# Graph attention on one core: 16 key blocks of each batch element turned by VectorE and DMA in place of TensorE

## The reference

```python
h = jnp.maximum(_layernorm(x, axis=-1), 0.0)
q = (h @ Wq + bq).reshape(b, n, H, HD)      # k, v alike; H, HD = 8, 64
scores = jnp.einsum('bihd,bjhd->bhij', q, k) / jnp.sqrt(jnp.float32(HD))
mask = jnp.where(adj == 0, jnp.float32(-1000000000.0), jnp.float32(0.0))
weights = jax.nn.softmax(scores + mask[None, None, :, :], axis=-1)
out = jnp.einsum('bhij,bjhd->bihd', weights, v)
return x + out.reshape(b, n, H * HD)
```

## Time and profile before

| | us |
|---|---|
| time, median of 3 runs | 3953.45 (3953.0 to 3953.62) |
| the profiled execution's own time | 3952.87 |
| its span, first to last instruction | 3951.1 |
| PE busy in the span | 3925.2 (99%) |
| DVE busy | 3109.3 (79%) |
| ACT busy | 3010.7 (76%) |
| DMA, share of 16 engines (queue 1) | 34.7% |

### The profile page before, as it was taken

How to read it: one execution, slowest core, us unless ns; L and a number is a source line. 1 busy time by engine, 2 the same in 40 slices (tenths; PEclk the granted TensorE clock), 3 DMA queues, 4 the chain that set the end, 5 groups by cost and what they waited for, 6 DMA issues and landing times.

```text
span 3951.1 us, 64302 instructions
## 1 busy us (share of the span) xinstructions
PE 3925.2 (99%) x21504; PEld 3219.8 (81%) x21504; DVE 3109.3 (79%) x5263; ACT 3010.7 (76%) x5386; POOL 1389.6 (35%) x1399
## 2 busy tenths in 40 slices
PE   8999999999999999999999999999999999999998
PEld 7888888888888888888888888888888888888887
DVE  7878878788787887878878788787887868878687
ACT  6877868778686886868868688686886868868687
POOL 4334333343333333333333333333333333334322
PEclk9999999999999999999999999999999999999999
DMA  6233333333323333334233342332433324324232
GB/s 208 60 88 72 88 78 67 85 79 80 83 66 83 89 70 84 73 75 95 63 84 80 68 96 65 82 84 62 96 73 75 87 61 94 80 67 90 51 76 49
DMA packets 722325, 316.44 MB, mean 80 GB/s; under 512 B 629840, under 2 KB 629840, under 8 KB 713424
## 3 DMA queue, kind: packets, MB, share of 16 engines
q1 hardware_dynamic: 722000, 312.34, 34.7%
HBM read 173.28 MB, written 38.27 MB: 54 GB/s over the span
## 4 chain that ended last, share of the span: by engine, by line
PE 92%; DVE 6%; issue 1%; ACT 1%; POOL 0%; DMA 0%; ACTq 0%; POOLq 0%; DVEq 0%
PE T L604 21%; PE misc L558 16%; PE S L589 11%; PE O L623 11%; PE S L590 11%; PE O L616 11%; PE misc L571 9%; DVE pT L909 2%; DVE S L903 1%; PE misc L537 1%; DVE bn L869 1%; DVE qB L886 1%; DVE y L928 0%; DVE qA L886 0%; ACT pT L722 0%
## 5 line engine op out<-in xcount | busy, mean ns | idle before, releaser
L909 DVE TENSOR_TENSOR pT<-T,pT 128x512 fp32r<-128x512 f32 x2048 | 1378.7, 686 | 657.1 <-ACT pT L722 651.5
L722 ACT CAST pT<-T 128x512 fp32r<-128x512 f32 x2048 | 1187.1, 590 | 412.8 <-PE T L604 326.1
L903 DVE CUSTOM_DVE_ANT_0 S<-S,mask 128x1024 f32<-128x1024 f32 x1024 | 1251.9, 1223 | 1.2 <-PE S L590 1.2
L604 PEld LDWEIGHTS T<-ident,probs 128*128 128x128 f32 x8192 | 996.9, 140 | 301.8 <-DVE pT L909 64.4
L604 PE MATMUL T<-ident,probs 128*128 128x128 f32 x8192 | 1236.5, 273 | 4.6 <-DVE pT L909 0.5
L741 ACT ACTIVATE probs<-S,negmax 128x1024 f32<-128x1024 f32 x1024 | 1150.7, 1124 | 7.0 <-DVE negmax L903 3.8
L623 PE MATMUL O<-pT,vs 128*64 128x512 f32 x2048 | 954.5, 466 | 0.2 <-DVE pT L909 0.2
L616 PE MATMUL O<-pT,vs 128*128 128x512 f32 x2048 | 816.1, 398 | 0.0
L558 PE MATMUL misc<-hT,wqk 128*128 128x512 f32 x3036 | 734.3, 391 | 0.0
L456 POOL TENSOR_TENSOR outs<-outs,oT 64x512 f32<-64x512 f32 x255 | 338.2, 1326 | 1024.4 <-DMA outs<-oT 1021.1
L558 PEld LDWEIGHTS misc<-hT,wqk 128*128 128x128 f32 x3036 | 570.0, 188 | 122.0 <-issue 0.2
(11 more groups left out here) (78 smaller groups left out, 3298.9 us busy)
## 6 DMA issues: line engine op xcount, KB each, us to landing
wqk<-wqk_split SPq DMA_DIRECT2D x63, 1024.0 KB, 6.0
xln<-in_x SPq DMA_DIRECT2D x240, 256.0 KB, 2.7
kA<-kA SPq DMA_DIRECT2D x128, 256.0 KB, 3.2
kB<-kB SPq DMA_DIRECT2D x128, 256.0 KB, 3.8
outs<-in_x SPq DMA_DIRECT2D x256, 128.0 KB, 3.6
outs<-oT SPq DMA_DIRECT2D x256, 128.0 KB, 3.6
out<-outs SPq DMA_DIRECT2D x252, 128.0 KB, 3.3
rinv_sq<-rinv_turned SPq DMA_DIRECT2D x512, 2.0 KB, 1.7
```

What stands on the lines that cost most here:

```text
L604: mm = pe.transpose(T[:, u % 2, i * P:(i + 1) * P], probs[:, (GB * g + i) % RING, j * P:(j + 1) * P], ident[:])
L722: act.copy(pT[:, u % PT, 0, :], T[:, u % 2, :]).then_inc(p_hi, 1)
L903: dve.tensor_tensor_reduce(S[:, s % 2, :], S[:, s % 2, :], mask[:, s % NB, :], 1.0, 3.0e38, ALU.add, ALU.min, negmax[:, s % RING:s % RING ...
L909: dve.tensor_tensor(pT[:, u % PT, 1, :], T[:, u % 2, :], pT[:, u % PT, 0, :].bitcast(F32), ALU.subtract).then_inc(p_lo, 1)
```

## The change

Of the 128 units of a batch 16 are no longer turned by TensorE. They go in 8 packs of two neighbouring units, listed in `PACKS` as (unit where VectorE starts, first unit of the pack): (0, 6), (6, 12), (38, 44), (70, 76), (102, 108), (121, 125), (126, 130), (127, 132), where 130 is unit 2 of the next batch. For each pack

- VectorE transposes the 32x32 squares of 128 x 1024 values of `probs` in one instruction (`turn_pack`) into a buffer of 512 KB. For the packs started at 121, 126, 127 and 0 the buffer is `xln`, for the others one part of `wv`, which is stored in DRAM once and loaded again at unit 110 of each batch (`load_wv`). There is one such buffer at a time, so `turn_pack` waits until the stores of the pack before have landed (`sq_out`);
- SyncE stores the squares to DRAM by four DMAs of 128 KB in pieces of 512 bytes (`store_pack`), waits for them at the next unit, and loads them back by two DMAs of 256 KB over the same place in `probs`, each 32x32 square now in its turned position (`load_pack`);
- ScalarE and VectorE take the high and the low part from `probs` (SBUF) in place of T (PSUM), through views of 4 x 4 x 32. In such a unit ScalarE takes the exponential before the high part. A group's ring slot is free when its turned units are turned and the moved ones' low part is made.

The first pack is left out in batch 0, the last four in batch 15: 123 packs, 246 units. The loads of the next x tiles move from unit 0 to unit 1 of SyncE's loop, behind the load of pack (0, 6). The order of TensorE's other work is as it was.

```diff
@@ -88,8 +88,46 @@
 XLN = 2
 SPREAD_0 = (2, 2, 6, 6, 6, 6, 8, 8)
 
+PACKS = ((0, 6), (6, 12), (38, 44), (70, 76), (102, 108), (121, 125), (126, 130), (127, 132))
+TWO = 2
+XLN_AT = 1
+WV_FREE, WV_AT = 2, 110
...
+def packs_of(b):
+    return [(k, at, slot) for k, (at, slot) in enumerate(PACKS)
+            if (b < B - 1 or at < (PAIRS - 1) * PER) and (b > 0 or at >= WV_FREE)]
...
+def pack_of(b, u):
+    for k, at, slot in packs_of(b):
+        if slot <= u < slot + TWO:
+            return pack_no(b, k), u - slot
+    if b > 0:
+        for k, at, slot in packs_of(b - 1):
+            if slot <= u + UNITS < slot + TWO:
+                return pack_no(b - 1, k), u + UNITS - slot
+    return None
...
@@ -203,6 +247,20 @@
             if not second:
                 return qA[:, :], kA[:, :, :]
             return qB[:, pair % 2, :], kB[:, pair % 2, :, :]
+        def probs_of(n, blocks=1):
+            g, j = n // NB, n % NB
+            at = GB * g % RING
+            return probs[:, at:at + GB, j * P:(j + blocks) * P]
...
+        def squares(at):
...
+            return wv_squares[:] if WV_FREE <= at < V_FROM else xln[:].rearrange("p t (j n) -> p (t j) n", n=P)
...
@@ -303,6 +361,32 @@
             for i in range(4):
                 sp.dma_start(adj_in_sb[:, 2 * i:2 * i + 2, :], adj_blocks[:, 2 * i:2 * i + 2]).then_inc(adj_in[i], 16)
 
+            def store_pack(b, k, at):
+                n, src = pack_no(b, k), squares(at)
+                sp.wait_ge(sq_turned, n + 1)
+                if some(n - 1):
+                    for i in range(TWO):
+                        sp.wait_ge(sq_in[i], 16 * (n - 1))
+                for a in range(QUADS):
+                    dst = turned_dram[n % 2, :, :, a, :].rearrange("j c n -> c j n")
+                    sp.dma_start(dst, src[a * SQ:(a + 1) * SQ]).then_inc(sq_out, 16)
+            def load_pack(b, k, slot):
+                n = pack_no(b, k)
+                sp.wait_ge(sq_out, 16 * QUADS * (n + 1))
+                for i in range(TWO):
+                    src = turned_dram[n % 2, QUADS * i:QUADS * (i + 1)].rearrange("q c a n -> (q c) a n")
+                    sp.dma_start(probs_of(UNITS * b + slot + i), src).then_inc(sq_in[i], 16)
+            def load_wv(b):
+                sp.wait_ge(sq_out, 16 * QUADS * pack_no(b, len([at for at, _ in PACKS if at < WV_AT])))
+                sp.wait_ge(wv_out, 16)
+                sp.dma_start(wv_shared, wv_dram).then_inc(wv_in, 16)
...
@@ -329,10 +415,6 @@
             def body(b, first=False, last=False):
                 for u in range(UNITS):
                     p, v = u // 32, u % 32
-                    if u == 0 and not first and not last:
-                        sp.wait_ge(h_turned, NB * (b + 1))
-                        for t in range(XLN):
-                            load_xln(b + 1, t)
...
+                    for i, k, at, slot in [(b, *it) for it in packs_of(b)] + [(b - 1, *it) for it in packs_of(b - 1) if b]:
+                        if UNITS * b + u == UNITS * i + at + 1:
+                            load_pack(i, k, slot)
+                    if u == XLN_AT and not first and not last:
+                        sp.wait_ge(h_turned, NB * (b + 1))
+                        sp.wait_ge(sq_out, 16 * QUADS * pack_no(b, len([at for at, _ in PACKS if at < WV_FREE])))
+                        for t in range(XLN):
+                            load_xln(b + 1, t)
...
@@ -369,6 +459,11 @@
                         if first and p < 2:
                             sp.wait_ge(wqk_stored[p + 2], 16)
                         load_wqk((p + 2) % PAIRS)
+                    for k, at, slot in packs_of(b):
+                        if u == at:
+                            store_pack(b, k, at)
+                    if u == WV_AT and not last:
+                        load_wv(b)
...
@@ -594,10 +691,15 @@
             def turn_probs(b, u):
 
                 n, g, j = UNITS * b + u, u // NB, u % NB
+                if pack_of(b, u):
+                    return
                 if j == 0:
                     pe.wait_ge(exped, GB * (GROUPS * b + g + 1))
-                if some(n - 1):
-                    pe.wait_ge(p_lo, n - 1)
+                last = n - 2
+                while last >= 0 and pack_of(*divmod(last, UNITS)):
+                    last -= 2
+                if last >= 0:
+                    pe.wait_ge(p_lo, last + 1)
                 else:
                     pe.wait_ge(v_biased, V_EARLY - 1 + n)
...
@@ -712,20 +814,31 @@
 
             def probs_hi(b, u):
                 n = UNITS * b + u
-                act.wait_ge(turned, n + 1)
+                moved = pack_of(b, u)
+                if moved:
+                    act.wait_ge(sq_in[moved[1]], 16 * (moved[0] + 1))
+                else:
+                    act.wait_ge(turned, turned_to(n))
                 if n == 0:
                     act.wait_ge(wqk_stored[1], 16)
 
                 used = n + 1 - (PT if u >= PT - 1 else PT - 1)
                 if some(used):
                     act.wait_ge(contracted, used)
-                act.copy(pT[:, u % PT, 0, :], T[:, u % 2, :]).then_inc(p_hi, 1)
+                if moved:
+                    act.copy(pT[:, u % PT, 0, :].rearrange("p (t a r) -> p a t r", t=GB, a=QUADS),
+                             probs_of(n).rearrange("p a (t r) -> p a t r", r=SQ)).then_inc(p_hi, 1)
+                else:
+                    act.copy(pT[:, u % PT, 0, :], T[:, u % 2, :]).then_inc(p_hi, 1)
...
+                    act.wait_ge(turned, turned_to(free - 1))
+                    moved = [m for m in range(free - NB, free) if pack_of(*divmod(m, UNITS))]
+                    if moved and s % GB == 0:
+                        act.wait_ge(p_lo, moved[-1] + 1)
...
@@ -833,12 +946,16 @@
                         copy_out(b - 1, GROUPS - 1)
                     if u > 1 and u % NB == 1:
                         copy_out(b, u // NB - 1)
-                    probs_hi(b, u)
+                    moved = pack_of(b, u)
+                    if not moved:
+                        probs_hi(b, u)
                     s = u // 2 + LEAD - 1
                     if u % 2 == 0 and s < SBLOCKS:
                         exponential(b, s)
                     if u % 2 == 0 and s >= SBLOCKS and not last:
                         exponential(b + 1, s - SBLOCKS)
+                    if moved:
+                        probs_hi(b, u)
...
@@ -905,9 +1022,26 @@
                                          negmax[:, s % RING:s % RING + 1]).then_inc(shifted, 1)
 
             def probs_low(b, u):
-                dve.wait_ge(p_hi, UNITS * b + u + 1)
-                dve.tensor_tensor(pT[:, u % PT, 1, :], T[:, u % 2, :], pT[:, u % PT, 0, :].bitcast(F32),
-                                  ALU.subtract).then_inc(p_lo, 1)
+                n = UNITS * b + u
+                dve.wait_ge(p_hi, n + 1)
+                if pack_of(b, u):
+                    hi, lo = (pT[:, u % PT, i, :].rearrange("p (t a r) -> p a t r", t=GB, a=QUADS) for i in (0, 1))
+                    dve.tensor_tensor(lo, probs_of(n).rearrange("p a (t r) -> p a t r", r=SQ), hi.bitcast(F32), ALU.subtract).then_inc(p_lo, 1)
+                else:
+                    dve.tensor_tensor(pT[:, u % PT, 1, :], T[:, u % 2, :], pT[:, u % PT, 0, :].bitcast(F32),
+                                      ALU.subtract).then_inc(p_lo, 1)
+            def turn_pack(b, k, at, slot):
+                n, pack = UNITS * b + slot, pack_no(b, k)
+                dve.wait_ge(exped, GB * (n // NB + 1))
+                if some(pack):
+                    dve.wait_ge(sq_out, 16 * QUADS * pack)
+                else:
+                    dve.wait_ge(wv_out, 16)
+                dve.transpose(squares(at).rearrange("p j (t r) -> p t j r", r=SQ),
+                              probs_of(n, TWO).rearrange("p t (j c) -> p t j c", c=SQ)).then_inc(sq_turned, 1)
...
@@ -996,6 +1130,9 @@
                     if u - 1 in HT_AT and not last:
                         h_low(b + 1, HT_AT[u - 1])
                     probs_low(b, u)
+                    for k, at, slot in packs_of(b):
+                        if u == at:
+                            turn_pack(b, k, at, slot)
                     s = u // 2 + LEAD
                     due = u % 2 == (1 if u // 2 * 2 in HALVED else 0)
```

20 lines of the change are left out of this document (18 added, 2 removed).

## The result

The changed kernel takes 3984.28 us (median of 4 runs, 3981.66 to 3987.96), beside 3953.22 for the kernel before on the same chip: ratio 1.008, 95% interval 1.0064 to 1.0096. It is slower by 31 us, where 39 us of gain were forecast, and it lies outside the range. Of the rivals on record the slower one has the sign, but its mechanism holds only part of the cause.

A forecast was written before the change was run, and what follows sets the result against it. TensorE was taken to bound the kernel, except where it waits for VectorE. Borders 17.3 plus pairs 2 and 3 24.8, less 3.2 and 0.2, gave 38.7 us off 3952.87: 3914 us, range 3872 to 3954.

The forecast's parts named there:

- The slower rival: Border: three transposes and two stores delay unit 1's projection; slower from 15.15 us on, 3958 or 3970 us; chance 0.11.
- -17.3 us at the borders: Borders of two batches, pack (6, 12) included: 15 borders gain 1.15 us each, 17.3 us.
- -21.4 in the pairs: Packs behind unit 6: pairs 2 and 3 gain 24.8 us, pair 1 loses 3.2, batch 0's pack (6, 12) loses 0.2.
- the walk: Border, followed operation by operation from unit 126: V projections wait 1.5 and 0.3 us in units 0 and 1.
- VectorE's place at unit 10: Behind the border: VectorE reaches unit 10's low part at about 2038.6 against 2040.02, 1.4 us ahead.
- A turn is worth 0.44 where TensorE binds: TensorE: a unit takes 0.90 us with a turn, 0.45 without; 246 units give at most 108.2 us.
- the sum of 0.8 twice: Pairs 2 and 3: VectorE follows most of two turns' 0.88 us, so each pack gains 0.8 us.
- Low parts from `probs`: 0.1 each taken: VectorE, moved units: a low part from SBUF paces at 0.72 us, from T 0.58; 0.1 us more each.
- The term of 0.2 per pack in pairs 0 and 1: VectorE's unbroken run: turns gain zero there and slower low parts of two units lose 0.2 us a pack.
- The link of two packs: Border: from a transpose's end to landed stores takes 4.4 us, bounds 4.1 and 5.6.
- the border's gain of 1.15: Border and pack (6, 12) together: 1.4 us ahead at unit 10, less 0.2 lost in units 12 and 13.
- The prediction called that transpose hidden: VectorE in unit 6 of a pair: the 1.25 us transpose fits 3.25 us of idle time; uncovered, 79 us.

The follow-up runs named there:

- e1: The changed kernel with one edit undone: in moved units ScalarE takes the high part before the exponential again; 3956.73 us, ratio 1.0009.
- e6: The kernel before with the turns of all 16 units a batch left out and nothing in their place; 3896.52 us, ratio 0.9858.
- e7: e4 with the moved units' high and low parts read from T in place of probs; 3934.52 us, ratio 0.9955.
- e4: The changed kernel with only the four packs behind unit 6 of each pair, high part before the exponential; 3946.13 us, ratio 0.9984.
- e3_border: The changed kernel with only the four border packs (started at 121, 126, 127 and 0), exponential still first; 3968.77 us, ratio 1.0043.
- e15_no_127: The changed kernel without pack (127, 132), high part before the exponential; 3954.76 us, ratio 1.0005.
- e8_spaced: The changed kernel with packs (0, 4), (70, 76), (102, 108), (121, 125), (126, 130) only, high part first; 3906.81 us, ratio 0.9884.
- e2: The changed kernel with only the four packs behind unit 6 of each pair, exponential still first; 3955.26 us, ratio 1.0006.
- e14_five: e8_spaced with pack (70, 76) moved to (70, 75), off unit 77; 3899.38 us, ratio 0.9865.
- e13: e14_five with packs (118, 123) and (2, 6) added; 3968.93 us, ratio 1.004.
- e16: e14_five with packs (78, 83), (86, 91) and (94, 99) added; 4112.88 us, ratio 1.0402.

## Why the prediction was wrong

Forecast: -17.3 us at the borders, -21.4 in the pairs. Measured with one half alone: +16 and +2, and 13 more together. Two steps failed most: the order on ScalarE, which the walk left out (27.5 us), and VectorE's place at unit 10, forecast 1.4 us ahead and measured 1.6 us late.

1. **The term that was never priced: the exponential ahead of the high part.** The prediction followed each pack on VectorE, SyncE and TensorE, and did not read ScalarE's new order in the moved even units at all. It costs 27.5 us (e1 against the changed kernel). It acts where a wait on VectorE can't be made up: in the runs of pairs 0 and 1, at the border, where the first transpose stands behind the low part of unit 126, and in pair 3, where the gain falls from 0.69 to 0.28 us (units 107-111).
2. **A turn is worth 0.44 where TensorE binds.** Right as a duration; but only 56 of 108 us can be had (e6). Pairs 0 and 1 give zero, as forecast from the earlier trace rows (e7: 0.02 in 7-18 and in 43-50). In pairs 2 and 3 the sum of 0.8 twice should have been 0.43 and 0.75: unit 77's turn is covered by another wait of TensorE. Beside the projections of V units 125 and 126 give 0.24 each and not 0.44.
3. **Low parts from `probs`: 0.1 each taken.** Its own rows give 0.72 - 0.58 = 0.14. The mean duration was 0.85 us against 0.69, and up to 1.82 beside GpSimd. The term of 0.2 per pack in pairs 0 and 1 is 0.3 (e7 against e4); what these reads cost at the border was not measured by itself. The prediction took the pace of one undisturbed operation and did not ask what GpSimd reads at that time.
4. **The link of two packs: 4.4 us taken, bounds 4.1 to 5.6.** The first was 3.8, the second 4.9 as the middle of 15 and over 6 in four borders, for which the sum had no term. The wait moved from the projection in unit 0 (0.7, not 1.5) to that in unit 1 (some 0.6 in a common border, up to 2.3 in the late ones, not 0.3). Their sum, 1.8 us a border, is the forecast's, but by luck: half of it comes from the exponential, and in e1 it is 0.9. This step did not decide.
5. **VectorE 1.4 us ahead at unit 10's low part.** This is the step that carried the border's gain of 1.15. The table is worked out from the traces: the start of VectorE's low part of a unit, less its start in the kernel before, counted from TensorE's difference at unit 123, mean of batches 2 to 13 (us; minus is ahead).

```
unit                2      6      8     10     18
changed          1.55   1.15   1.72   1.58   2.33
e3_border        1.87   1.39   1.11   0.98   0.98
e1_high_first    0.65  -0.21   0.56   0.42   1.31
e15_no_127      -0.93  -1.38   0.12  -0.02   1.13
e8_spaced       -0.93  -1.42  -1.84  -1.97  -1.96
e6_turns_out    -0.92  -1.91  -2.40  -2.53  -2.53
```

With no added work VectorE would be 2.53 us ahead at unit 10, which is all that TensorE keeps of its own 3.16; it is 1.58 late. Of the 4.1 us between them the order on ScalarE is 1.2 (e1), pack (127, 132) is 0.4 (e15), and 1.95 lie between e15 and e8: the transpose in unit 6, and units 6 and 7 moved in place of 4 and 5. The prediction called that transpose hidden, by the idle time of unit 102. Alone in pair 0 it is (e2 loses nothing before unit 12), but behind the border VectorE has no such idle time. From unit 10 to 18 come 0.35 from the reads of (6, 12) and the falls of the clock.
6. **The slower rival** asked for a chain of three transposes and two stores over 15.15 us. It measured 1.24 x 3 + 3.7 + 6.4 = 13.8 in the border shown and some 1.4 us less in a common one, below its own point of decision, and the kernel was slower all the same. So its mechanism, though at work (e15: 1.6 us a batch), did not decide.
7. **The clock, put at nothing.** In the kernel before TensorE's granted clock does not fall before the last unit; the profiled execution of the changed kernel has four, three behind units 12 and 13 of pair 0 and one at unit 126. The three cost 1.5 us each (4.3 against 2.8 us in units 7 to 18). The other three executions have a mean clock of 0.996 against 0.999, so up to 0.003 x 3984 = 12 us of the 31 may be clock. e1 and e15 have 0.996 and 0.997; e2, e4 and e6 have 0.999.
8. **What held**: the count of turns, the transpose of 1.24, the stores' 2.3 to 2.9 us (the 2.3 that the prediction worked out from the Trainium skill, "DMA: Bandwidth & Descriptors", Anatomy of one DMA, rests on a fit to DMAs issued by GpSimd; SyncE's stores from `wv_squares` agree with it), the reload of V's weights and of x without a wait worth naming, and the late turn of units 16 and 48 for VectorE, though 0.81 us and not 1.2.

The best version found is e14_five, 3899.38 us: 10 units moved instead of 16, high part first, 1.35% below the kernel before. It has nearly all that e6 showed to be there (53 of 56 us), because four of its six missing units (12, 13, 44, 45) stood where a turn is worth nothing, and the other two, 6 and 7, are worth 0.4 us a batch in e6.

What stays open: of the 60 us between e6 and e1, 48 lie between e15 and e8, but how they split between the transpose in unit 6, the reads of units 6 and 7 beside GpSimd and the clock is not shown: e8 changes all of them at once, and no kernel was run that keeps the transposes and leaves out only the transfers.

## What to carry to other kernels

Price a piece of work by the engine that is waited for at that place: leave it out first and measure (e6), before building what replaces it; half of these turns could never have paid. When a change hands work to another path, read the order inside every engine that the path crosses, and every transfer already queued there. A cover read in one place, such as idle time in front of an operation, must be read again in every place where it is used, with the delays that the change itself brings. In a stretch where a second engine runs without a break, time saved ahead of it comes back only if that engine too has less to do.

## What the hardware showed that was not expected

- **The granted clock falls after waits in mid-run.** It fell to half, 1.2 GHz, in the middle of the run. In the changed kernel, after two waits of 1.14 and 0.81 us close together (timeline and windows of it):

```profile
580.92 0.44 PE L725 MATMUL O<-pT,vs 128*64 128x512 f32 x1 [1.14 <-DVE pT L1029]
...
582.41 0.63 PE L706 MATMUL T<-ident,probs 128*128 128x128 f32 x4 [0.81 <-DVE pT L1031]
...
585.07 1.05 PE L706 MATMUL T<-ident,probs 128*128 128x128 f32 x4
```

```profile
575.00:580.00 5.00, 4.78 (x26) 3.68 (x24) 4.90 (x8) 3.83 (x9) 2.61 (x4) 1.00 0.16 52
580.00:585.00 5.00, 3.27 (x12) 2.33 (x13) 4.69 (x10) 3.16 (x7) 2.98 (x5) 0.83 0.20 52
585.00:590.00 5.00, 5.00 (x28) 4.19 (x27) 3.50 (x6) 3.22 (x6) 2.93 (x3) 0.83 0.64 144
```

  Four transposing matmuls take 1.05 us there, 0.60 elsewhere. The same waits stand in every batch, and the clock fell in three of them; what decides it is not shown. The mean clock was 0.999 before, 0.998 in the profiled execution of the changed kernel, 0.996 in e13 and 0.987 in e16, so that in e16 up to 0.012 x 4114 = 49 us of its 160 may be clock and not wait.
- **VectorE and GpSimd hold each other up** where both of VectorE's operands are in SBUF (0.69 to 1.82 us on VectorE, 1.29 to 1.73 on GpSimd), and not where one is in PSUM; the rows stand with e7.
- **A store of 128 KB in pieces of 512 bytes lands in 2.3 us** (the median of `wv_squares`; 2.9 for those from `xln`, of which some stand behind loads), as fast as one of 8 KB. At the border the landing can come late without the DMA engines being busy: in the border shown they are busy 10% from 2034.0 to 2036.5 us, and VectorE is released at 2036.5. The transposing view of four dimensions, 1.24 us for 128x1024, is no slower than two plain ones of 128x512 (2 x 0.709 us).
